# Laying a token's two expert results by expert number, and adding the lower ones to the residual on VectorE

## The reference

```
topw, topi = top_k(softmax(x @ rw + rb), 2);  topw = softmax(topw)
out = sum over the two chosen experts e of  topw_e * (gelu(x @ w1[e] + b1[e]) @ w2[e] + b2[e])
x   = layernorm(x + out) * ln3_g + ln3_b
```

## Time and profile before

| | before |
|---|---|
| median of 3 runs (lowest, highest) | 982.85 us (981.31, 984.86) |
| the profiled execution | 977.55 us |
| its span, first to last instruction | 975.8 us |
| mean granted clock of TensorE | 0.986 |
| output projection behind the attention (L957) starts | 673.9 us |
| main loop over experts | 743 to 942 us |
| end (mixing, layer norm, stores) | 942 to 975.8 us |

### The profile page before, as it was taken

One profiled execution on the slowest core, in us unless ns is written; L12 is line 12 of the kernel. 1 busy time (PEld: TensorE's weight loads), 2 busy tenths in 40 slices (PEclk: granted clock), 3 DMA queues, 4 the chain that ended last, 5 costly groups with the idle time before them and its releaser, 6 DMA issues.

```text
span 975.8 us, 18808 instructions
## 1 busy us (share of the span) xinstructions
PE 943.1 (97%) x5812; PEld 551.2 (56%) x5813; DVE 593.7 (61%) x1006; ACT 557.3 (57%) x1164; POOL 341.0 (35%) x465
## 2 busy tenths in 40 slices
PE   7899999999999999999999999998998999999995
PEld 4456543533445445333543334234898999999974
DVE  4657798788777887787787788863431211212226
ACT  3354566677765656777666766785343444444442
POOL 3465853534325435313446036112441111111115
PEclk9799999999999999999999999998999999999998
DMA  7363323213114111201624022002231344334225
GB/s 218 99 168 81 92 78 97 56 45 92 43 52 115 50 66 34 66 2 41 215 92 149 4 69 64 12 21 62 44 116 39 118 129 124 120 106 140 49 75 199
DMA packets 93899, 84.04 MB, mean 86 GB/s; under 512 B 37638, under 2 KB 87302, under 8 KB 93702
## 3 DMA queue, kind: packets, MB, share of 16 engines
q1 hardware_dynamic: 85436, 63.93, 23.6%
q0 software_dynamic: 5360, 16.82, 5.0%
q10 hardware_dynamic: 3040, 2.49, 1.0%
HBM read 38.63 MB, written 12.63 MB: 53 GB/s over the span
## 4 chain that ended last, share of the span: by engine, by line
PE 87%; PEld 3%; DVE 3%; DMA 2%; POOL 1%; issue 1%; ACT 1%; PEldq 0%; ACTq 0%; POOLq 0%; DVEq 0%
PE o_bank L946 16%; PE a_bank L929 16%; PE v_slot L893 11%; PE v_slot L1433 11%; PE a_bank L1427 9%; PE a_bank L858 6%; PE a_bank L876 4%; PE v_slot L897 4%; PE v_slot L957 3%; PE o_bank L1427 3%; PE v_slot L898 2%; PEld a_bank L1427 1%; DVE max_q L1116 1%; PEld v_slot L1433 1%; DMA b_sa_bk<-in_sa_bk 1%
## 5 line engine op out<-in xcount | busy, mean ns | idle before, releaser
L1062 ACT ACTIVATE probs<-a_bank 128x512 f32<-128x512 f32 (+1 forms) x688 | 360.3, 591 | 143.4 <-PE a_bank L929 138.0
L1116 DVE TENSOR_REDUCE max_q<-v_slot 128x1 f32<-128x1024 f32 (+3 forms) x352 | 397.8, 1169 | 69.6 <-PE v_slot L893 43.6
L929 PE MATMUL a_bank<-q_stack_cross,k_stack_cross 99*128 99x512 bf16 x512 | 162.8, 381 | 0.6 <-ACT probs L1062 0.3
L1439 ACT ACTIVATE hidden<-a_bank,b 128x128 f32<-128x128 f32 x216 | 79.1, 367 | 144.4 <-PE a_bank L1427 132.8
L893 PE MATMUL v_slot<-k_stack_cross,q_stack_cross 96*128 96x512 bf16 x512 | 148.5, 379 | 0.2 <-DVE max_q L1116 0.2
L1433 PE MATMUL v_slot<-stack_or_weights,hidden 128*128 128x256 f32 x576 | 130.3, 379 | 0.0
L946 PE MATMUL o_bank<-probs,v_cross 128*32 128x512 f32 x1024 | 129.5, 601 | 0.0
L1433 PEld LDWEIGHTS v_slot<-stack_or_weights,hidden 128*128 128x128 f32 x576 | 106.7, 190 | 13.0
L1427 PE MATMUL a_bank<-x_col,stack_or_weights 128*128 128x128 f32 x864 | 109.8, 277 | 2.6 <-issue 2.6
L929 PEld LDWEIGHTS a_bank<-q_stack_cross,k_stack_cross 99*128 99x128 bf16 x512 | 45.3, 97 | 118.4 <-ACT probs L1062 67.0
L1427 PEld LDWEIGHTS a_bank<-x_col,stack_or_weights 128*128 128x128 f32 x864 | 105.9, 194 | 4.9 <-issue 3.2
(11 more groups left out here) (215 smaller groups left out, 1084.3 us busy)
## 6 DMA issues: line engine op xcount, KB each, us to landing
k_stack_cross<-parts SPq DMA_DIRECT2D x96, 128.0 KB, 2.4
stack_or_weights<-in_e_w SPq DMA_DIRECT2D x12, 1024.0 KB, 6.5
stack_or_weights<-parts SPq DMA_DIRECT2D x91, 128.0 KB, 2.4
q_stack_cross<-parts SPq DMA_DIRECT2D x48, 128.0 KB, 2.4
inputs<-in_ctxT POOLq DMA_DIRECT2D x4, 1024.0 KB, 6.1
stack_or_weights<-in_e_w SPq DMA_DIRECT2D x8, 512.0 KB, 5.2
x_slots<-slots_in SPq DMA_DIRECT2D x116, 32.0 KB
y_got<-token_out SPq DMA_DIRECT2D x11, 256.0 KB, 8.1
```

The lines of the kernel that those rows point to most:

```text
L929: last = nc.tensor.matmul(bank[:, i * cols:(i + 1) * cols], lhs, q_stack[kind][0:KM, G * u + j, q0:S], start=True, stop=True)
L1062: nc.scalar.activation(probs[tile % PB][:, js[0]:js[-1] + 1, q0:S], a_bank[at % AS][:, 0:len(js) * (S - q0)].rearrange("p (j t) -> p j t", ...
L1116: nc.vector.tensor_reduce(most, rows, X, ALU.max, negate=True).then_inc(v_free, 1)
L1439: nc.scalar.activation(hidden[:, f, :], h_bank[f % HB][:, 0:P], ACT.Gelu, bias=b1[:, bass.ds(e * FC + f, 1)]).then_inc(flow.gelu_done, 1)
```

## The change

The meaning of the two halves changes: column `D + 1` now holds the *lower* of a token's two expert numbers (a minimum instead of a copy), so half 0 of `token_out` holds the result of the lower expert and half 1 that of the upper. A lower result never comes from the last expert.

- `choose` gets one comparison (`is_lt`, column 7 of `top_val`); `finish` gets seven more small steps that sort the two weights by expert number, in both places where it runs.
- SyncE loads the eight lower halves as soon as all tiles before the last expert's have landed, and behind the last tile the upper halves of groups 0, 2, 4, 6 and 7; ScalarE loads those of 1, 3 and 5, behind the last four diagonals.
- VectorE gets `blend`: two scalar_tensor_tensor instructions for each group, residual + weight x lower result, for groups 0 to 5 ahead of the last batch's weights, for 6 and 7 behind them.
- TensorE's `came_in(n)` waits for `blend(n)` and comes behind the wait for the last tile; of the mixing products half remain (the upper results). ScalarE makes 16 diagonals instead of 32.

The core of the diff:

```diff
-BY_SCALAR = 5
+BY_SCALAR = (1, 3, 5)
...
+                     vec.tensor_tensor(top_val[:, t0:t0 + n, 7], self.idx_f[:, 0, :], self.idx_f[:, 1, :], ALU.is_lt))
...
-                vec.tensor_copy(x2_all[:, self.t0:self.t0 + n, D + 1], self.idx_f[:, 0, :]).then_inc(slots_ready, 1)
+                vec.tensor_tensor(x2_all[:, self.t0:self.t0 + n, D + 1], self.idx_f[:, 0, :], self.idx_f[:, 1, :], ALU.min).then_inc(slots_ready, 1)
...
-                vec.tensor_tensor(self.second_w, self.first_w, self.step, ALU.mult).then_inc(top_w_ready, 1)
+                self.done(dve, vec.tensor_tensor(self.second_w, self.first_w, self.step, ALU.mult))
+
+                self.done(dve, vec.tensor_tensor(self.sum, self.first_w, self.first_lower, ALU.mult))
+                self.done(dve, vec.tensor_tensor(self.step, self.second_w, self.first_lower, ALU.mult))
+                self.done(dve, vec.tensor_tensor(self.first_w, self.first_w, self.sum, ALU.subtract))
+                self.done(dve, vec.tensor_tensor(self.second_w, self.second_w, self.step, ALU.subtract))
+                self.done(dve, vec.tensor_tensor(self.step, self.step, self.first_w, ALU.add))
+                self.done(dve, vec.tensor_tensor(self.first_w, self.second_w, self.sum, ALU.add))
+                vec.tensor_copy(self.second_w, self.step).then_inc(top_w_ready, 1)
...
+            sp.wait_ge(main.y_stored, first * 16)
+            sp.sem_inc(passed, 1)
+            for n in range(TT // FT):
+                load_results(sp, n, 0)
+
             sp.wait_ge(main.y_stored, (first + count) * 16)
             sp.sem_inc(passed, 1)
-
             for n in range(TT // FT):
-                load_results(sp, n, 0)
-                if n >= BY_SCALAR:
+                if n not in BY_SCALAR:
                     load_results(sp, n, 1)
...
-            for n in range(7):
-                came_in(n)
...
-            came_in(7)
-
             for n in range(TT // FT):
-                pe.wait_ge(mix_ready, 2 * max(LAST_BATCH, FT * (n + 1)))
-                pe.wait_ge(got[n], 32)
+                pe.wait_ge(blended, n + 1)
+                came_in(n)
+
+            for n in range(TT // FT):
+                pe.wait_ge(mix_ready, max(LAST_BATCH, FT * (n + 1)))
+                pe.wait_ge(got_upper[n], 16)
...
             sc.wait_ge(top_w_ready, 2)
-            for t in range(LAST_BATCH, LAST_BATCH + 2):
-                for k in range(2):
-                    diagonal(k, t)
+            for t in range(LAST_BATCH, TT):
+                diagonal(t)
...
-            for n in range(BY_SCALAR):
+            for n in BY_SCALAR:
                 load_results(sc, n, 1)
...
+            def blend(n):
+                dve.wait_ge(got_lower[n], 16)
+                for t in range(n * FT, (n + 1) * FT):
+                    last = nc.vector.scalar_tensor_tensor(x2_all[:, t, 0:D], y_got[:, t, 0, :], top_val[:, t, 5:6], x2_all[:, t, 0:D], ALU.mult, ALU.add)
+                last.then_inc(blended, 1)
+
+            dve.wait_ge(top_w_ready, 1)
+            for n in range(LAST_BATCH // FT):
+                blend(n)
             last_weights.steps_apart(dve)
             last_weights.finish(dve)
+            dve.wait_ge(top_w_ready, 2)
+            for n in range(LAST_BATCH // FT, TT // FT):
+                blend(n)
```

More of the change, by code:

```diff
@@ L532, in __init__ @@
                 self.n, self.number, self.steps = t1 - t0, number, before
-                self.second, self.sum, self.step, self.first_w, self.second_w = (top_val[:, t0:t1, c] for c in range(2, 7))
+                self.second, self.sum, self.step, self.first_w, self.second_w, self.first_lower = (top_val[:, t0:t1, c] for c in range(2, 8))
             def done(self, dve, ins):
@@ L1318, in decoder_layer @@
         scattered_late = sem("scattered_late")
-        got = [sem(f"got{n}") for n in range(TT // FT)]
+        got_lower = [sem(f"got_lower{n}") for n in range(TT // FT)]
+        got_upper = [sem(f"got_upper{n}") for n in range(TT // FT)]
+        blended = sem("blended")
         mix_ready, mixed = sem("mix_ready"), sem("mixed")
@@ L1569, in _ @@
                     load_all(2 * pair + i + 2)
-            first = sp.value_load(first_i[0:1, E - 1:E], min_val=0, max_val=SLOT_TILES)
+            first = sp.value_load(first_i[0:1, E - 1:E], min_val=1, max_val=SLOT_TILES)
             count = sp.value_load(tiles_i[0:1, E - 1:E], min_val=1, max_val=TOK // P)
@@ L1649, in _ @@
             pe.sem_inc(passed, 1)
-            came_in(7)
             for n in range(TT // FT):
-                pe.wait_ge(mix_ready, 2 * max(LAST_BATCH, FT * (n + 1)))
-                pe.wait_ge(got[n], 32)
+                pe.wait_ge(blended, n + 1)
[3 more added lines that the diff above has]
+                pe.wait_ge(got_upper[n], 16)
                 for i in range(FT):
                     t = n * FT + i
-                    for k in range(2):
-                        last = nc.tensor.matmul(mix_bank[n][:, i * D:(i + 1) * D], mix[:, k, t, :], y_got[:, t, k, :], start=False, stop=(i == FT - 1 and k == 1))
+                    last = nc.tensor.matmul(mix_bank[n][:, i * D:(i + 1) * D], mix[:, t, :], y_got[:, t, 1, :], start=False, stop=(i == FT - 1))
                 last.then_inc(mixed, 1)
@@ L1676, in _ @@
                     expert_tiles(sc, main, 2 * pair + i, lambda g, _: activate_tile(sc, main, 2 * pair + i, g))
-                    for k in range(2):
-                        diagonal(k, 2 * pair + i)
-                    diagonal(i, pair + E)
+                    diagonal(2 * pair + i)
+                    if i == 0:
+                        diagonal(pair + E)
             last_weights.exps(sc)
@@ L1689, in _ @@
             sc.sem_inc(passed, 1)
-            for n in range(BY_SCALAR):
+            for n in BY_SCALAR:
                 load_results(sc, n, 1)
-            for t in range(LAST_BATCH + 2, TT):
-                for k in range(2):
-                    diagonal(k, t)
             def scale_back(n):
```

17 lines of the change are left out of this document (8 added, 9 removed).

## The result

The changed kernel takes 984.54 us in the median (982.15 to 987.16), the kernel before, measured beside it, 981.98 (975.60 to 986.07). The ratio is **1.0037, with a 95% interval of 1.0022 to 1.0053**, that is 3.6 us (2.2 to 5.2); the plain difference of the medians, 2.56 us, lies in that interval. Slower, then, by about what was forecast. The profiled execution after has a span of 982.8 us, that of before 975.8. These 7 us are not all the change's: 2.5 of them stand already at 669.92 (667.39 in the earlier trace rows), ahead of both places that the prediction names, after a granted clock of 0.57 in 20 to 40 us where before had 0.74. Of the change only three of the four small steps in `choose` lie ahead of that point.

The account below looks back on a forecast made before the run. TensorE is busy for 943.1 of 975.8 us, but VectorE bounds two places, behind the attention and at the end. First weights 1.54 + end 2.2 = 3.7 us on 982.85 gave 986.6 us, range 984.0 to 989.8.

Parts of the forecast that it names:

- both places that the prediction names: VectorE's two critical places: behind the attention, ahead of the output projection; and the end, up to group 1's statistics.
- First weights, seven more steps: Ahead of the output projection: seven dependent VectorE steps of 0.22 us, 1.54 us all on the path; what follows shifts whole.
- Blends, last weights and loads: At the end: six blend pairs take 4.74 us, ScalarE loads 6.28 us later, group 1's statistics +1.2 us.
- TensorE's clock: At the end: about 2.7 us idle lowers the clock for 4 us; group 1's statistics +2.2 us instead of +1.2.
- rival A: At the end: the clock holds, so the sum is 2.7 us, 985.6 us; chance 0.27.
- The factor of 1.87: In the clock term: sixteen products of 256 columns took 6.49 us at low clock, 3.47 at full clock.
- Lower loads under the last expert, removed work: Eight lower loads have 17 us and meet a store, counted 0 (bound 1.6 us); removed products and diagonals mostly hidden.
- C: Under the last expert: loads delay a store and TensorE, up to 1.6 us more; 989.5 us; chance 0.10.
- D: At the end: lower halves not there at 942.66, blends wait, up to 3 us more; 989.6 us; chance 0.02.
- B: At the end: blends and steps closer together than any row shows, not slower; 982.9 us or below; chance 0.04.

Follow-up runs that it names:

- e10: Kernel before plus seven extra small steps behind each of the two sets of weights, and all sixteen result loads on SyncE; ratio 1.0019.
- e12: Kernel before with all 16 loads of results issued by SyncE, no steps added; ratio 1.0001.
- e1: Changed kernel with the first weights' seven sorting steps moved later on VectorE, into its idle time behind the first early tile's transpose; ratio 1.0021.
- e5: Changed kernel with the first weights' sorting steps moved later and all upper halves loaded by SyncE; ratio 1.0017.
- e9: Changed kernel run and profiled once more, no edit; ratio 1.0036.
- e3: Changed kernel with SyncE loading all eight upper halves, none left to ScalarE; ratio 1.0023.
- e8: Kernel before with only the last batch's weights made ahead of the main loop; ratio 0.9995.
- e2: Changed kernel with three spare products on TensorE between the sixth and seventh copy of the residual; ratio 1.0044.
- e4: Kernel before with seven more small steps, results unused, behind each of the two sets of weights; ratio 1.0074.

## Why the prediction was right

*First weights, seven more steps.* Right in length: 1.54 us forecast, +1.51 of idle time, 1.50 between e10 and e12. That what follows shifts whole is not borne out. From the projection to the last `y_row` it took 267.96 us before and 268.79 after, but that these are so near is luck. Up to the first product of the main loop (743.08, 749.57 below) after took 2.46 us more, in part for two waits that before's profile lacks and all others have. Timeline of after, TensorE from 677 to 760 us:

```profile
725.93 1.60 PE L1438 MATMUL a_bank<-x_col,stack_or_weights 128*128 128x128 f32 x12 [0.39 <-ACT hidden L1450]
...
734.48 1.60 PE L1438 MATMUL a_bank<-x_col,stack_or_weights 128*128 128x128 f32 x12 [1.26 <-ACT hidden L1450]
```

In the loop, where its clock stayed whole, after took 1.63 less. And without the steps ahead of the projection TensorE can wait for `x_col` later: 0.28 us in e1, 0.61 in e5, 0.83 in e12. Less these waits, the steps cost 1.1 us (e9 against e1), 0.7 or 0.8 (e3 against e5, e10 against e12), and the full 1.5 only against before and e8, where the projection ran longer (6.33 us to the next product; 5.24 to 5.74 in e1, e5 and e12) and no such wait shows.

*Blends, last weights and loads.* Right in the mechanism and near in every length: six pairs took 4.84 us (4.74 forecast), so 0.79 a pair from start to start; ScalarE asked 5.9 us later against the landmark (6.28); its first two loads landed in 2.7 and 3.0 us (2.7), the third in 3.7. Where the load alone decides (e9, e1, e2), group 1 is 1.0 us late (1.2 forecast); with the load given to SyncE 0.5 (0.5 to 0.8). The Trainium skill, "VectorE: DVE Perf Modes", section on the TRN2 errata, leads with its 58 cycles to shorter steps and blends and to an estimated sum of 0.9 us; the rows of after show 0.22 and 0.79 a pair again, and the measured 3.6 us are four times that sum. The same section says that its row with the 58 cycles under-predicts the duration of a single instruction and names a measured fixed term of about 150 cycles; that gives an estimated 0.17 us for a step and 0.42 for a blend, and the durations here are 0.18 and 0.48.

*TensorE's clock.* Right for the profiled execution: a gap of 2.46 us (2.7 forecast), the clock low for some 3.4 us behind it (4), group 1 at +2.19 instead of +2.2. But the step treats as settled for the kernel what differs between its executions. In e9 the same program ended with +1.0, the end of rival A, because the clock had fallen earlier and was whole again. Forecast and A are not two ways that the kernel could go, of which one is true: both occur, from execution to execution, and the late fall is the rarer one here (one profile of five). So that 3.7 us came out as 3.6 is in part luck. (The factor of 1.87 sets 6.49 us of the timeline against 3.47 of the chain; in the timeline alone sixteen such products of the loop take 3.62, a factor of 1.79, which changes the +2.2 by 0.1.) The row that the step rested on, a fall behind 2.55 us of idling at 740.5, shows it too. After has the same idle time at the same place, here in its timeline and in the stretch ahead, and there the clock stayed:

```profile
749.57 1.60 PE L1438 MATMUL a_bank<-x_col,stack_or_weights 128*128 128x128 f32 x12 [2.55 <-issue]
```

```profile
750.00:900.00 150.00, 150.00 (x1032) 141.32 (x1031) 31.45 (x106) 66.60 (x182) 20.19 (x21) 1.00 0.39 109
```

All fourteen profiles have this wait, 2.53 to 2.56 us long. In ten of them the clock is at 0.50 within the next four microseconds, and the loop takes 198.54 to 198.79 us; in after, e2, e8 and e12 it stays at 1.00, and the loop takes 197.15 to 197.98.

The ratios of 1.0037 and 1.0036 lie nearer the forecast's 3.7 us than A's 2.7, but their intervals hold both.

*Lower loads under the last expert, removed work.* Right: all eight, begun by 933.7 and landed in at most 6.1 us, were there when the blends began (947.60), and the store beside them landed after 940.30 - 933.88 = 6.42 us, as in the earlier trace rows (6.43), without idling on TensorE. Rivals C and D are out. B is out by the lengths above. What the prediction didn't weigh is the other side of the change: e4 shows that its steps alone would have cost 4.0 us at the end, in the old order of loads. That the earlier lower loads and the single late load of a group give back most of that, so that the end lost only 1.0 to 2.1 us, fits these numbers, but no run takes them alone.

## What to carry to other kernels

A few small steps cost their own length only where nothing else stands behind them: look at what the engine that waits for them does next, and if that is issuing transfers that others need, give these to an engine that waits for nothing. Work that waits for no late data (here the last weights) belongs ahead of the loop, and while one engine takes work over from another, the idle one should get a share of it. Before a term is built on the clock falling behind a gap, look whether the same gap falls in a second execution.

## What the runs showed of the hardware

- The granted clock after the same wait of the same code differs between executions: behind 2.53 to 2.56 us of idling ahead of the main loop it fell to 0.50 in ten of fourteen profiles (before among them) and stayed at 1.00 in four (after among them); behind 1.96 us ahead of the first copy it stayed at 1.00 in after, and behind 1.97 it was 0.50 in e9. A fall ahead of the loop goes with a loop that is 0.6 to 1.6 us longer.
- A 256 KB load took 5.2 us when ScalarE issued it 1.5 us behind SyncE's first of eleven (e4), and 2.7 when it was issued some 4 us behind SyncE's last (after).
